# Two-job groups in a row, the maximum pass six jobs ahead, and the last block of a head unrolled

## The reference

```python
q = (x @ Wq + bq)            # 1600 queries, 16 heads of 16 numbers
k, v = cond @ Wkv + bkv      # 16*1444 = 23104 keys
q, k, v = _fq_sym(q), _fq_sym(k), _fq_sym(v)
attn = softmax(einsum('bhqd,bhkd->bhqk', q, k))
attn = _fq_unsigned(attn)    # steps of (row maximum)/255, so a row's largest score is needed first
out  = einsum('bhqk,bhkd->bhqd', attn, v)
```

## Time and profile before

| what | value |
|---|---|
| time, median of 3 runs | 8865.77 us (8865.53 to 8866.54) |
| profiled execution, its own time | 8868.33 us |
| its span, first to last instruction | 8866.5 us |
| PE busy | 8204.1 us (93%) |
| DVE busy | 6557.1 us (74%) |
| ACT busy | 5411.8 us (61%) |
| POOL busy | 5204.3 us (59%) |
| mean granted PE clock | 0.952 |

### The profile page before, as it was taken

The page is one execution under the profiler, slowest core; times in us unless marked ns, Lnnn a source line. Parts: engine busy times, 40 slices in busy tenths (PEclk is TensorE's granted clock), DMA queues, the critical chain, the costliest instruction groups (busy, mean ns, idle before and its releaser), DMA issues.

```text
span 8866.5 us, 223893 instructions
## 1 busy us (share of the span) xinstructions
PE 8204.1 (93%) x60312; PEld 2566.4 (29%) x60312; DVE 6557.1 (74%) x6161; ACT 5411.8 (61%) x12138; POOL 5204.3 (59%) x3573
## 2 busy tenths in 40 slices
PE   8934899999999999999999999999999999988588
PEld 4510222222222222222222222222222222222343
DVE  8969877777777777777777777777777777710466
ACT  2300576767676767676767676767667676777233
POOL 5724465656565656565656565656656565666356
PEclk9955899999999999999999999999999999999789
DMA  5663002020202020202020202010111111010100
GB/s 162 209 136 114 14 13 33 12 34 12 35 11 34 12 34 12 34 12 34 12 34 12 34 11 34 12 28 19 26 20 25 21 22 24 18 24 7 26 4 4
DMA packets 305414, 303.94 MB, mean 34 GB/s; under 512 B 50718, under 2 KB 297802, under 8 KB 300458
## 3 DMA queue, kind: packets, MB, share of 16 engines
q1 hardware_dynamic: 304682, 303.13, 15.6%
q10 hardware_dynamic: 672, 0.16, 0.0%
HBM read 226.31 MB, written 76.71 MB: 34 GB/s over the span
## 4 chain that ended last, share of the span: by engine, by line
PE 84%; DVE 6%; issue 5%; POOL 2%; ACT 1%; DMA 1%; SPq 0%; DVEq 0%; ACTq 0%; POOLq 0%
PE psum L1378 30%; PE psum L1347 26%; PE psum L1303 15%; PE psum L1357 6%; DVE mpart L1166 3%; PE psum L1268 2%; ACT y L1065 1%; POOL mix L411 1%; PE psum L671 1%; PE psum L1337 1%; DVE act_c L551 1%; PE psum L1405 1%; POOL kq L924 1%; POOL kq L931 1%; PE psum L644 0%
## 5 line engine op out<-in xcount | busy, mean ns | idle before, releaser
L1166 DVE TENSOR_REDUCE mpart<-psum 128x978 f32 x4992 | 5655.3, 1172 | 1414.0 <-PE psum L1303 1341.0
L1065 ACT ACTIVATE y<-psum 128x400 f32<-128x400 f32 x11520 | 5007.0, 506 | 2063.2 <-PE psum L1378 1971.0
L985 POOL TENSOR_SCALAR xh<-y 128x1600 f16<-128x1600 f32 x2880 | 4397.9, 1527 | 2747.2 <-PE psum L1357 1554.1
L1378 PE MATMUL psum<-QT,K 99*128 x11520 | 3180.6, 341 | 68.3 <-ACT y L1065 55.7
L1347 PE MATMUL psum<-y,ones 128*17 128x400 f32 x23048 | 2537.3, 507 | 0.0
L1303 PE MATMUL psum<-K,QS 48*128 48x489 bf16 x9984 | 1768.6, 390 | 288.5 <-DVE mpart L1166 194.0
L1378 PEld LDWEIGHTS psum<-QT,K 99*128 x11520 | 875.6, 97 | 2618.2 <-issue 2477.0
L1357 PE MATMUL psum<-xh,vwin 128*16 128x400 f16 x11528 | 1019.2, 335 | 0.7 <-POOL xh L985 0.7
L1303 PEld LDWEIGHTS psum<-K,QS 48*128 48x128 bf16 x9984 | 433.4, 93 | 1553.6 <-issue 1074.7
L1347 PEld LDWEIGHTS psum<-y,ones 128*17 128x17 f32 x23048 | 401.7, 95 | 651.6 <-ACT y L1065 386.0
L1357 PEld LDWEIGHTS psum<-xh,vwin 128*16 128x16 f16 x11528 | 321.8, 90 | 624.9 <-issue 397.9
(11 more groups left out here) (180 smaller groups left out, 2153.6 us busy)
## 6 DMA issues: line engine op xcount, KB each, us to landing
K<-kT_parts SPq DMA_DIRECT2D x204, 240.0 KB, 8.3
vwin<-v_int SPq DMA_DIRECT2D x579, 80.0 KB, 1.9
K<-kT_parts SPq DMA_DIRECT2D x772, 45.8 KB
kT_parts<-part SPq DMA_DIRECT2D x135, 256.0 KB, 3.3
K<-kT_parts SPq DMA_DIRECT2D x102, 242.0 KB, 8.3
src<-in_ctx_dram SPq DMA_DIRECT2D x46, 512.0 KB, 4.6
v_float<-kv SPq DMA_DIRECT2D x45, 512.0 KB, 5.2
vin<-v_float SPq DMA_DIRECT2D x9, 2560.0 KB, 12.7
```

The source lines that it names most:

```text
L985: pool.tensor_scalar(xh[:, g % YR, :, :], y[:, g % YR, :, :], INT_STEP, 0.0, ALU.mult, ALU.add)\
L1065: act.activation(y[:, s % YR, j, :], s2_bank(GT * s + j), ACT.Exp).then_inc(exp_done, 1)
L1166: dve.tensor_reduce(mpart[:, t, ds(2 * cp + j, 1)], s1_buf(n)[:, :, 0:CHALF], AX.XY, ALU.max)\
L1378: pe.matmul(s2_bank(t), K3[0:MROW, h % 2, ds(c * REGION + t * P, P)], queries, start=True, stop=True).then_inc(s2_ready, 1)
```

## The change

The jobs of a body are put at other places. Groups 0 to 9 and group 14 have two jobs, groups 10 to 13 have one, and no group is split. The last six jobs of a body (`LEAD`) belong to the next body's key piece, and a body's own piece is finished after its job 20 (`OWN`), in group 9. The first six jobs of all are done ahead of the main stage. SP's loads of `K1` and `QS` follow the new order.

The last block of each head is written out as three bodies, without its inner loop. In its last body the maxima of head `h + 1` are taken inside: on DVE ahead of the job of group 10, with PE's transpose in group 12 (`TURN_AT`) ahead of its job, and ACT's copy and DMA ahead of the third exponential of that group. The turn of a block moves from group 6 to group 13. In `sum_group` one wait on `exp_done` goes away.

```diff
-SINGLE = (2, 6, 10, 14)
-JOBS_AT = [1 if s in SINGLE else 2 for s in range(GROUPS)]
-SPLIT = (1, 4, 8, 12)
+JOBS_AT = [2] * 10 + [1] * 4 + [2]
+LEAD_AT, TURN_AT = 10, 12
+LEAD = sum(JOBS_AT[LEAD_AT:])
+OWN = JOBS - LEAD
-EPI_SLOT = 6
+EPI_SLOT = 13
@@ bodies
-                with eng.Fori(0, BLOCKS) as b:
+                with eng.Fori(0, BLOCKS - 1) as b:
                     body(h, b, 0, True)
                     with eng.Fori(1, BODY_C) as c:
                         body(h, b, c, True, later=True)
-                body(h, None, None, True)
+                body(h, BLOCKS - 1, 0, True)
+                for c in range(1, BODY_C):
+                    body(h, BLOCKS - 1, c, True, later=True, final=c == BODY_C - 1)
@@ SP, next_values
-                        after_job(base + QT_TILES - 1)
+                        after_job(base + QT_TILES - LEAD - 1)
                         load_k1(head % H, nxt % BODIES, 0)
                     if not last and q == 1 and head_end:
-                        after_job(base + QT_TILES + QS_PARTS[0][1] - 1)
+                        after_job(base + QT_TILES + QS_PARTS[0][1] - LEAD - 1)
                         load_qs((h + 2) % H, 0)
-                    if not last and q == 2:
-                        after_job(base + JOBS - 1)
+                    if not last and q == 1:
+                        after_job(base + OWN - 1)
                         load_k1(head % H, nxt % BODIES, 1)
                         if head_end:
                             load_qs((h + 2) % H, 1)
@@ ACT
+                        if final and s == TURN_AT and j == 2:
+                            mt_copy(h + 1, s1_at(h, b, c, True) + 2 + sum(JOBS_AT[:TURN_AT]))
@@ DVE, ahead of the main stage
+            for n in range(LEAD):
+                job(0, n % QT_TILES, n // QT_TILES, BODIES * JOBS + 2, n)
@@ DVE, body
+                        if final and s == LEAD_AT:
+                            maxima(h + 1, at + n)
+                        if final and s == TURN_AT:
+                            n += 2
                         for _ in range(JOBS_AT[s]):
-                            job(BODY_C * b + c, done % QT_TILES, done // QT_TILES, at, n)
+                            lead = done >= OWN
+                            cp = (0 if final else BODY_C * b + c + 1) if lead else BODY_C * b + c
+                            k = done - OWN if lead else done + LEAD
+                            job(cp, k % QT_TILES, k // QT_TILES, at, n)
@@ PE, ahead of the main stage
+            for n in range(LEAD):
+                job(1, 0, n % QT_TILES, n // QT_TILES, BODIES * JOBS + 2, n, first=True)
@@ PE, sum_group
-                if g >= 0:
-                    pe.wait_ge(exp_done, S2_RING + T + GT * (g + 1))
@@ PE, next_jobs and the group
+                        if done < OWN:
+                            k = done + LEAD
+                            job(h + 1, BODY_C * b + c, k % QT_TILES, k // QT_TILES, at, done + extra, first=not later)
+                        else:
+                            k = done - OWN
+                            job(h + 2 if final else h + 1, 0 if final else BODY_C * b + c + 1, k % QT_TILES,
+                                k // QT_TILES, at, done + extra, first=final)
-                    next_jobs(1 if s in SPLIT else JOBS_AT[s])
+                    if final and s == TURN_AT:
+                        maxima(h + 1, at + done)
+                        extra = 2
+                    next_jobs(JOBS_AT[s])
                     score_tile(s, 2)
                     score_tile(s, 3)
-                    if s in SPLIT:
-                        next_jobs(1)
```

More of the change, by code:

```diff
@@ L91 @@
 SLOTS_HEAD = BLOCKS * SLOTS_BLOCK + 2
-assert sum(JOBS_AT) == JOBS and CSIZE % 2 == 0 and DUP == 64
+assert sum(JOBS_AT) == JOBS and sum(JOBS_AT[:TURN_AT]) % 2 == 0 and CSIZE % 2 == 0 and DUP == 64
 assert Q_STEPS + 1 + RING * LOOP_N <= STEPS - 2
-EPI_SLOT = 6
+EPI_SLOT = 13
 ITEMS = FC * E
@@ L345, in body_of @@
             return BODIES * h + BODY_C * b + c
-        PRO_SLOTS = BODIES * JOBS + 2
+        PRO_SLOTS = BODIES * JOBS + 2 + LEAD
         def s1_at(h, b, c, pass1):
@@ L970, in _, with body @@
             pool.wait_ge(ring_init, 2)
-            def body(h, b, c, pass1, later=False):
-                if b is None:
-                    return
+            def body(h, b, c, pass1, later=False, final=False):
                 if not later:
@@ L1032, in mt_copy @@
                 act.dma_start(QT[NROW:MROW, head % 3, :].rearrange("r (t c) -> r t c", c=P), mT[:]).then_inc(m_in, 16)
-            mt_copy(0, PRO_SLOTS - 2)
+            mt_copy(0, BODIES * JOBS)
             act.wait_ge(vx_stored, 16)
@@ L1201, in _ @@
                     job(cp, n % QT_TILES, n // QT_TILES, JOBS * cp, n)
-            maxima(0, PRO_SLOTS - 2)
+            maxima(0, BODIES * JOBS)
+            for n in range(LEAD):
+                job(0, n % QT_TILES, n // QT_TILES, BODIES * JOBS + 2, n)
             def outputs(B, at, n):
@@ L1339, in turn_out, with sum_group @@
                 last.then_inc(s1_ready, 2)
-            def sum_group(T, g, start):
-                if g >= 0:
-                    pe.wait_ge(exp_done, S2_RING + T + GT * (g + 1))
+            def sum_group(g, start):
                 for j in range(GT):
@@ L1383, in next_jobs @@
                     for _ in range(count if pass1 else 0):
-                        job(h + 1, BODY_C * b + c, done % QT_TILES, done // QT_TILES, at, done + extra, not later)
+                        if done < OWN:
[5 more added lines that the diff above has]
+                                k // QT_TILES, at, done + extra, first=final)
                         done += 1
@@ L1406, in body @@
                             .then_inc(summed_x, 1)
-                        sum_group(T, 0, True)
+                        sum_group(0, True)
                     if later or g != 0:
-                        sum_group(T, g, False)
+                        sum_group(g, False)
                     g = s - LAG_PV
@@ L1434, in _ @@
             for g in range(-LAG_SUM, 0):
-                sum_group(0, g, False)
+                sum_group(g, False)
             for g in range(-LAG_PV, 0):
```

## The result

| | before | after |
|---|---|---|
| median of 7 runs each, us | 8866.54 | 8897.49 |
| lowest and highest, us | 8865.53, 8870.42 | 8888.91, 8904.17 |
| ratio, with its 95% interval | | 1.0034 [1.0024, 1.0044] |
| profiled execution: own time, us | 8868.3 | 8904.17 |

The changed kernel is slower, by 31 us. The forecast was 8865, "no change" the likeliest; the range held the time.

The account below looks back on a forecast made before the run. The prediction took PE, busy for 93% of the span, to bound the kernel. Terms of +76, -78 and +1 us sum to -1 on the profiled 8868.3, given as 8865 us on the median; range 8820 to 8931.

Parts of the forecast that it names:

- the head's end: Between heads: 9.5 us a head go and 4.3 replace them, -78 us over 15 heads.
- ahead of the main stage: Six jobs before the main stage, paced by DVE in a gap that waits for QT: tail costs about +1 us.
- Doubles in a row: Consecutive two-job groups: every second one stalls for DVE, 2.66 and 2.38 us in turn, 1.26 a block, +76 us.
- The maxima inside the last body: Groups 10 to 12 of a head's last body: chain ends at 3.9 us, group 12's job at 7.07, costing 2.1 a head.
- The jump back: PE's head loop, now five bodies: if not held, the jump waits for code; bounds 0 and 3.8 us, 1.9 taken.
- the jump is dear: Rival at the head's end: jump costs 3.8 us and the clock falls, 2.5 more; 8931 us, chance 0.20.
- The written-out bodies: Unrolled bodies of each head's last block have constants for c in place of a register; nothing taken for that.
- The wait in `sum_group`: Removed wait on exp_done: costs nothing, as score tile 2 of the same group asked for that count before.
- the turn of the block: Moved to group 13: costs and saves the same, a longer group and a following double waiting for DVE's normalization.
- K1: SP's moved key loads: over 3 us left before use; if late, 1 us a body would be 180 us, not expected.
- the free jump's rival: Rival at the head's end: the jump back costs nothing; 8836 us, or 8822 if the maxima miss POOL; chance 0.22.

Follow-up runs that it names:

- e1_doubles: The kernel before with only the job order changed (two jobs in groups 0 to 9 and 14, one in 10 to 13, no split): 8937.48 us, ratio 1.0080.
- e4_hint: The changed kernel plus a prefetch hint that the head's loop will jump back, nothing else different: 8818.99 us, ratio to before 0.9945.
- e8_merge: e4_hint with DVE's reduces written to fixed columns of a small tile, merged into the running maximum once a body: 8785.22 us, ratio to before 0.9908.
- e11_heads3: The changed kernel with three heads written out in each turn of the head loop, no hint: 8834.14 us, ratio to before 0.9960.
- e6_sumwait: e4_hint with the removed wait of sum_group put back: 8820.55 us, ratio to before 0.9946.
- e7_epi6: e4_hint with the turn of a block moved back from group 13 to group 6: 8817.3 us, ratio to before 0.9945.
- e3_unroll: The kernel before with only the last block of each head written out as three bodies, maxima still behind it: 8855.03 us, ratio 0.9987.

## Why the prediction was wrong

The sum was +76 for the doubles, -78 for the head's end, +1 ahead of the main stage. Measured on the profiled execution it is +36 (8904.2 against 8868.3). Term by term:

- **Doubles in a row: right.** 2.67 and 2.38 in turn were predicted as 2.66 and 2.38; PE's waits for DVE at the job rose from 394 to 688 us. In e1_doubles the order alone makes a head 462.1 - 457.4 = 4.8 us longer, against 4 x 1.26 = 5.0 in the text. In the changed kernel a block in the loop is 1.3 to 1.4 longer, by the starts of its groups.
- **The maxima inside the last body: right but for the clock.** `maxima` began 0.78 us after group 10's first tile (0.85 predicted) and its last instruction ended at 3233.17, 3.91 behind it (3.9). POOL's instruction of 3231.59 held it, 1.37 us for a kind that takes 0.17 alone, as the earlier trace rows had shown of L1175. The job of group 12 went at 6.94 (7.07), and the group takes 4.13 us for 2.26 where the clock stays up: 1.9 for the 2.1 of the text. e4_hint, without the jump's stall, keeps this stall of group 12. The page "SBUF — State Buffer" of the Trainium skill, section Who interferes with whom, says this of two-input DVE instructions; the trace agrees. That section also names casts, and L1193 of e8_merge, a cast of 13 elements that took 1.42 us and ended with POOL, agrees.
- **The jump back: the step that failed.** The text took 1.9 us for it, one load of the nearest kind, 15 times, and nothing for the clock. The jump measured 3.8 at the median (2 x 1.9 was the upper bound), 14 times, and the clock fell to 1.2 GHz behind it. By e4_hint the two cost 5.6 us each, by e11_heads3 6.3: 79 to 88 us where the sum had 28.5, so 50 to 60 too few. That PE no longer holds the head's loop was the right side of the text's "if that isn't held", as the instruction packets now show. The mechanism was the rival "the jump is dear", whose 3.8 and 2.5 are close; the error was to put it at 0.20 because "the gap would be half as long". A gap half as long was still enough for the clock to fall. The Trainium skill, "Runtime: NRT & Kernel Launch", section Instruction fetch mechanics, says that a taken jump to code outside the window must fetch before it goes on. The trace agrees, with 3.3 to 3.9 us on PE in the runs without the hint.
- **A smaller slow stretch, put at nothing too.** Behind the stall of group 12 the granted clock was 0.50 as well (the first window row above), in 11 of 15 heads: 1.4 us each, some 15 us, of which 10 are already in the 50 to 60 above, because e4_hint has the stretch in only 4.
- **The written-out bodies: taken at nothing, they give back.** A stalled double is 0.14 shorter in them (2.53 for 2.67), a single 0.06 (2.26 for 2.32). By the starts of the groups, the written-out block of the changed kernel is 2.3 us shorter than one in the loop, its slow stretch left aside: 34 us in 15 heads. The column's register explains 0.10 of the 0.14 (e8_merge); the rest stays open.
- **The wait in `sum_group`, the turn of the block: right, nothing** (e6_sumwait, e7_epi6).
- **Ahead of the main stage** the six jobs cost about 2 us, not 1: from the first copy of the maxima to the first score tile it is 6.9 us against 5.1.
- **K1** loaded earlier is not waited for in the main stage: the jobs' two waits for a load of keys (73.0 us in all, 71.7 before) lie ahead of it.

Against the forecast that makes 50 to 60 for the jump, 5 for the rest of the slow stretch, up to 7 for the doubles, 1 ahead of the main stage and 34 back: +22 to +39, where +37 was measured. That the time lies inside the range, between the forecast and the dear rival's 8931, is partly luck: a gain that the text had put at nothing covers more than half of the jump that it had too cheap. Without the jump's stall the changed kernel would have been at 8819, 46 below the forecast and 17 below the free jump's rival.

## What to carry to other kernels

Before a loop body is written out, ask whether its code will still be held when the loop jumps back; instruction packets in a later turn, and the duration of the branch, show it. If not, price the jump with the clock that falls behind it, count the jumps that are really taken, and give the hint or make the jumps fewer. A wait put down to a busy engine can also be shortened at its start: look at how long after its release the instruction begins, and at whether a register gives its address.

## What the runs showed of the hardware that was not expected

- A taken jump to code that PE doesn't hold: 3.3 to 3.9 us in the changed kernel, e3_unroll and e11_heads3; held: 0.21; not held, but with the hint: 0.38.
- A gap of 4 us on PE was enough for the clock to fall to 1.2 GHz (PEclk 0.50 in the window from 3248); behind a gap of 0.57 us in e4_hint it stayed at 2.4 (1.00).
- Behind waits of 1.19 and 0.49 us in one group, the window from 3237 to 3240 shows 0.50 too, though PE was busy in between; the window from 2317 to 2320, behind the same two waits, shows 1.00.
- A DVE reduce whose output column comes from a register starts 0.53 us after the job's first matmul, one with a fixed column 0.42.
